# A third stack buffer, one merge transfer, a reordered sync queue, and rotary swaps issued by GpSimd

## What is computed

```python
x = x + tanh(g_xattn[0]) * xattn(layernorm(x), ctx_2048, ...)
x = x + tanh(g_ffn[0]) * ffn(layernorm(x), ...)

def xattn(x, c):                      # 16 batches of (128 channels, 512 positions)
    q, k, v = Wq @ x + bq, Wk @ c + bk, Wv @ c + bv      # 8 heads of 16 channels
    q, k = rope(q, 8), rope(k, 8)     # the first 8 channels of a head are rotated
    p = softmax(q.T @ k / sqrt(16))
    return Wo @ (p @ v) + bo

def ffn(x):                           # weights 4 bit, unpacked and scaled in the kernel
    gate, up = split(x @ w_gate_up.T)
    y = (silu(gate) * up) @ w_down.T
    return y / sqrt(mean(y * y) + 1e-6)
```

## Time and profile before

| | us |
|---|---|
| median of 3 runs | 921.22 |
| lowest and highest run | 918.21, 933.62 |
| the profiled execution | 918.37 |
| its span, first to last instruction | 916.6 |
| PE, DVE, ACT, POOL busy | 815.8, 522.1, 483.6, 178.5 |
| DMA engines' mean busy share | 33% |

### The profile page before, as it was taken

How to read it: one execution, slowest core, us unless ns; L and a number is a source line. 1 busy time by engine, 2 the same in 40 slices (tenths; PEclk the granted TensorE clock), 3 DMA queues, 4 the chain that set the end, 5 groups by cost and what they waited for, 6 DMA issues and landing times. The chain is left out here.

```text
span 916.6 us, 13653 instructions
## 1 busy us (share of the span) xinstructions
PE 815.8 (89%) x5110; PEld 421.6 (46%) x5142; DVE 522.1 (57%) x760; ACT 483.6 (53%) x895; POOL 178.5 (19%) x174
## 2 busy tenths in 40 slices
PE   3378999999998988999993599999999999999997
PEld 1123333333333333334332376666666666666664
DVE  4398977888987867888871961314131423141113
ACT  2227776887787766778792552325231623252223
POOL 1232333333333423331112820000000000000000
PEclk8559999999999988999996889999999999999999
DMA  5678555666665666465212010002000110000001
GB/s 167 171 198 218 155 142 153 189 200 194 170 165 152 175 175 189 119 167 153 69 33 79 8 46 1 1 1 67 25 1 1 47 45 0 0 27 21 0 1 46
DMA packets 55176, 86.44 MB, mean 94 GB/s; under 512 B 19274, under 2 KB 20938, under 8 KB 55114
## 3 DMA queue, kind: packets, MB, share of 16 engines
q1 hardware_dynamic: 55114, 85.62, 33.0%
HBM read 44.70 MB, written 34.34 MB: 86 GB/s over the span
## 5 line engine op out<-in xcount | busy, mean ns | idle before, releaser
L670 DVE TENSOR_REDUCE neg_max<-s_ps 128x2 f32<-128x1024 f32 x256 | 310.0, 1219 | 61.8 <-PE s_ps L420 60.8
L536 ACT ACTIVATE probs<-st_ps 128x512 f32<-128x512 f32 x512 | 277.9, 597 | 105.5 <-PE st_ps L432 101.2
L448 PE MATMUL pv_ps<-probs,v_ones 128*32 128x256 f32 x2048 | 166.1, 397 | 12.6 <-ACT pv_sb L542 12.6
L1098 PE MATMUL gu_ps<-x_head,gu_head 128*128 128x512 f32 x352 | 155.9, 443 | 0.0
L965 DVE TENSOR_TENSOR hidden<-gu_ps,silu 128x512 f32<-128x512 f32 x44 | 30.4, 691 | 202.6 <-ACT silu L1040 202.6
L420 PE MATMUL s_ps<-k_stack,q_stack 48*128 48x512 f32 x512 | 135.4, 526 | 10.5 <-DVE neg_max L670 8.4
L1099 PE MATMUL gu_ps<-x_rest,gu_head 128*128 128x512 f32 x352 | 139.0, 395 | 0.0
L1040 ACT ACTIVATE silu<-gu_ps 128x512 f32<-128x512 f32 x44 | 26.3, 597 | 204.8 <-PE gu_ps L1101 204.8
L432 PE MATMUL st_ps<-q_stack,k_stack 50*128 50x512 f32 x512 | 110.6, 421 | 12.9 <-DMA q_stack<-max_scratch 12.7
L420 PEld LDWEIGHTS s_ps<-k_stack,q_stack 48*128 48x128 f32 x512 | 50.4, 193 | 121.1 <-issue 81.1
L1115 PE MATMUL y_ps<-dn_head,h_head 128*128 128x512 f32 x176 | 101.5, 577 | 1.1 <-DVE h_rest L967 1.0
(11 more groups left out here) (114 smaller groups left out, 807.1 us busy)
## 6 DMA issues: line engine op xcount, KB each, us to landing
q_stack<-image SPq DMA_DIRECT2D x64, 192.0 KB, 3.9
k_stack<-image SPq DMA_DIRECT2D x64, 192.0 KB, 4.5
image<-split_head SPq DMA_DIRECT2D x32, 256.0 KB
image<-split_head SPq DMA_DIRECT2D x64, 128.0 KB
image<-split_rest SPq DMA_DIRECT2D x32, 256.0 KB
ct<-ctx_dram SPq DMA_DIRECT2D x16, 256.0 KB, 5.5
swap<-proj SPq DMA_DIRECT2D x64, 64.0 KB, 2.0
scale_of<-inverse_scratch SPq DMA_DIRECT2D x16, 256.0 KB
```

Of the source, the lines that this page charges most:

```text
L448: last = nc.tensor.matmul(pv_ps[2 * KC * j:2 * KC * (j + 1), cols], v_ones[b % 2][:, kt, j, quad, :], probs[at % PROBS][:, j, cols], start ...
L536: nc.scalar.activation(probs[at % PROBS][:, tile % 4, :], st_ps[item % ST_BANKS][:], ACT.Exp).then_inc(st_read, 1)
L670: nc.vector.tensor_reduce(neg_max[j // 2][:, :, j % 2, qt], s_ps[item % S_BANKS][:], AXIS_X, ALU.max, negate=True).then_inc(s_read, 1)
L1098: nc.tensor.matmul(gu_ps[t % 2][:, half], head, x_head[:, k], start=(k == 0), stop=False)
```

## The change

- `q_stack` and `k_stack` get three buffers (`STACKS`) instead of two. `load_stacks` reads a whole batch at once in four transfers of 384 KB, where `load_half` read 4 x 192 KB twice. It waits for all eight stores of its batch, and stands first in `sync_step` for batch b+2. It waits for the last `weigh` of batch b-1.
- The stores are `store_heads` (six transfers) and `store_rests` (two), both halves together. They stand at the end of `sync_step`, with `gather_sums(b, 0)` between them.
- On VectorE one cast of 128x1024 (`split_heads`, after slot 11) takes the place of `head_pass` (slot 7) and `head_rot` (slot 11); on GpSimd one subtract (`split_rests`) takes the place of two. `rotate` now leaves its result in `proj`, so `bias_rot` of the next batch waits for `rests`.
- The four swap transfers are issued by GpSimd in `pool_step`, after `residual` and before `rotate`.
- The rows of the two halves of the heads are interleaved, so `merge_quads` is one transfer over every second row instead of four, `store_inverse` one instead of two, and `load_inverse` two (one per half of the heads) instead of one.
- At the start, ScalarE does the scales, the gates and their table loads ahead of `bias_rot(2)`; GpSimd issues the first swaps once all constants are in, where SP issued them after the gates' transfers.

The core of the diff; `take_v`, `values`, `weigh`, `score` and the host's weight order only follow the new layout and buffer count.

```diff
-X_TILES, C_TILES, PROBS = 8, 4, 3
-MIX_AT, ROT_AT, PASS_AT, V_AT = 1, 2, 5, 8
+X_TILES, C_TILES, PROBS, STACKS = 8, 4, 3, 3
+MIX_AT, ROT_AT, PASS_AT, V_AT, HEADS_AT = 1, 2, 5, 8, 11
...
-            def swap_partners(sp, n):
-                sp.wait_ge(st_read, ST_NO["rot", n] + 1)
+            def swap_partners(pool, n):
+                pool.wait_ge(st_read, ST_NO["rot", n] + 1)
                 if n:
-                    sp.wait_ge(rot_rest, n)
+                    pool.wait_ge(rests, n)
                 for at in range(0, P, 64):
                     for to, source in ((at, at + 32), (at + 32, at)):
-                        sp.dma_start(swap[to:to + 32, :], proj[source:source + 32, 0, :]).then_inc(swapped, 16)
-
-            def store_head(sp, n, w):
-                sp.wait_ge((rot_head, pass_head)[w], n + 1)
-                rows = lambda first, count: image[n, first:first + STEP_ROWS * count:STEP_ROWS].rearrange("r h t -> r (h t)")
-                tile = split_head[:, w, :].bitcast(F32)
-                sp.dma_start(rows(3 * w + 1, 16), tile).then_inc(stored[w], 16)
-                sp.dma_start(rows(3 * w, 8), tile[halves[0]]).then_inc(stored[w], 16)
-                sp.dma_start(rows(K_ROW0 + 3 * w + 2, 8), tile[halves[1]]).then_inc(stored[w], 16)
-
-            def store_rest(sp, n, w):
-                sp.wait_ge((rot_rest, pass_rest)[w], n + 1)
-                rows = image[n, 3 * w + 2:3 * w + 2 + STEP_ROWS * 16:STEP_ROWS].rearrange("r h t -> r (h t)")
-                sp.dma_start(rows, split_rest[:, w, :].bitcast(F32)).then_inc(stored[w], 16)
-
-            def load_half(sp, n, h):
-                p = n % 2
+                        pool.dma_start(swap[to:to + 32, :], proj[source:source + 32, 0, :]).then_inc(swapped, 16)
+
+            def store_heads(sp, n):
+                sp.wait_ge(heads, n + 1)
+                tile = split_head[:].bitcast(F32)
                 for w in two:
-                    sp.wait_ge(stored[w], PARTS * (n + 1))
-                if n >= 2:
-                    sp.wait_ge(st_full, last_weight(n - 2, h))
+                    sp.dma_start(image_rows(n, 3 * w + 1, 16), tile[:, w, :]).then_inc(stored, 16)
+                    sp.dma_start(image_rows(n, 3 * w, 8), tile[halves[0], w, :]).then_inc(stored, 16)
+                    sp.dma_start(image_rows(n, K_ROW0 + 3 * w + 2, 8), tile[halves[1], w, :]).then_inc(stored, 16)
+
+            def store_rests(sp, n):
+                sp.wait_ge(rests, n + 1)
+                for w in two:
+                    sp.dma_start(image_rows(n, 3 * w + 2, 16), split_rest[:, w, :].bitcast(F32)).then_inc(stored, 16)
+
+            def load_stacks(sp, n):
+                sp.wait_ge(stored, PARTS * (n + 1))
+                if n >= STACKS:
+                    sp.wait_ge(st_full, last_weight(n - STACKS, 1))
                 for stack, row0 in ((q_stack, 0), (k_stack, K_ROW0)):
                     for odd in two:
-                        rows = stack[p][STACK * odd:STACK * odd + DATA_ROWS, columns(h), :].bitcast(F32)
-                        heads = slice(odd * PAIRS + 2 * h, odd * PAIRS + 2 * h + 2)
-                        sp.dma_start(rows, image[n, row0:row0 + DATA_ROWS, heads, :]).then_inc(half_in[p][h], 16)
+                        rows = stack[n % STACKS][STACK * odd:STACK * odd + DATA_ROWS, :, :].bitcast(F32)
+                        sp.dma_start(rows, image[n, row0:row0 + DATA_ROWS, odd * PAIRS:(odd + 1) * PAIRS, :]).then_inc(
+                            stack_in[n % STACKS], 16)
...
             def merge_quads(sp, b):
                 sp.wait_ge(sums_in[0], 16 * (b + 1))
-                for j in range(QUAD):
-                    rows = slice(2 * KC * j + KC, 2 * KC * (j + 1))
-                    sp.dma_start(pv_sb[0][b % 2][rows, :], pv_sb[1][b % 2][rows, :]).then_inc(merged[b % 2], 16)
+                sp.dma_start(pv_sb[0][b % 2][1:P:2, :], pv_sb[1][b % 2][1:P:2, :]).then_inc(merged[b % 2], 16)
 
             def store_inverse(sp, b):
                 sp.wait_ge(inverses, b + 1)
-                for h in two:
-                    sp.dma_start(inv_dram[b, :, h, :], sums[64 * h:64 * h + 64, :]).then_inc(inverse_out, 16)
+                sp.dma_start(inv_dram[b].rearrange("h j (x e) -> (h j x) e", e=32), sums[:]).then_inc(inverse_out, 16)
 
             def load_inverse(sp, b):
-                sp.wait_ge(inverse_out, 16 * QUADS * (b + 1))
+                sp.wait_ge(inverse_out, 16 * (b + 1))
                 if b:
                     sp.wait_ge(heads_ok, b)
-                sp.dma_start(scale_of[:], inv_dram[b].rearrange("j h t -> (j h) t").unsqueeze(1).to_broadcast(
-                    [HEADS, KC, T])).then_inc(inverse_in, 16)
+                for h in two:
+                    sp.dma_start(scale_of[h:P:2, :], inv_dram[b, h].unsqueeze(1).to_broadcast([QUAD, KC, T])).then_inc(inverse_in, 16)
...
             def sync_step(sp, b):
                 nxt, proj_n = b + 1 < B, b + AHEAD_PROJ
-                if nxt:
-                    load_half(sp, b + 1, 1)
+                if b + 2 < B:
+                    load_stacks(sp, b + 2)
                 store_max(sp, b, 1)
-                if proj_n < B:
-                    swap_partners(sp, proj_n)
                 if b:
                     gather_sums(sp, b - 1, 1)
+                load_max(sp, b, 1)
+                if b:
                     merge_quads(sp, b - 1)
-                load_max(sp, b, 1)
                 if b >= 2:
                     store_x(sp, b - 2)
                 if b:
                     store_inverse(sp, b - 1)
-                if proj_n < B:
-                    store_head(sp, proj_n, 1)
-                if b + 2 < B:
-                    load_half(sp, b + 2, 0)
                 if nxt:
                     store_max(sp, b + 1, 0)
+                if b + 5 < B:
+                    load_inputs(sp, b + 5)
                 if b:
                     load_inverse(sp, b - 1)
-                if proj_n < B:
-                    store_rest(sp, proj_n, 1)
-                if b + 5 < B:
-                    load_inputs(sp, b + 5)
                 if nxt:
                     load_max(sp, b + 1, 0)
+                if proj_n < B:
+                    store_heads(sp, proj_n)
                 gather_sums(sp, b, 0)
                 if proj_n < B:
-                    store_head(sp, proj_n, 0)
-                    store_rest(sp, proj_n, 0)
+                    store_rests(sp, proj_n)
...
-                swap_partners(sp, 0)
                 sp.dma_start(gu_sc16[:], d["gate_up_scales"].rearrange("g (t o) -> (g t) o", o=P)).then_inc(scales_in, 16)
                 sp.dma_start(dn_sc16[:], d["down_scales"].rearrange("g (t o) -> (g t) o", o=P)).then_inc(scales_in, 16)
-                store_head(sp, 0, 1)
-                store_rest(sp, 0, 1)
-                store_head(sp, 0, 0)
-                store_rest(sp, 0, 0)
-                sp.wait_ge(ones_set, 2)
-                for h in two:
-                    load_half(sp, 0, h)
-                swap_partners(sp, 1)
+                store_heads(sp, 0)
+                store_rests(sp, 0)
+                sp.wait_ge(ones_set, STACKS)
+                load_stacks(sp, 0)
                 load_inputs(sp, 3)
-                for w in (1, 0):
-                    store_head(sp, 1, w)
-                    store_rest(sp, 1, w)
-                load_half(sp, 1, 0)
+                store_heads(sp, 1)
+                store_rests(sp, 1)
+                load_stacks(sp, 1)
                 store_max(sp, 0, 0)
-                swap_partners(sp, 2)
                 load_max(sp, 0, 0)
                 load_inputs(sp, 4)
-                for w in (1, 0):
-                    store_head(sp, 2, w)
-                    store_rest(sp, 2, w)
+                store_heads(sp, 2)
+                store_rests(sp, 2)
...
-                engine.wait_ge(rot_head, n + 1)
+                ops.tensor_tensor(proj[:, 0], swap[:], turned[:], ALU.add).then_inc(rotated, 1)
+
+            def split_rests(engine, ops, n):
+                engine.wait_ge(heads, n + 1)
                 if n:
-                    engine.wait_ge(stored[0], PARTS * n)
-                ops.tensor_tensor(split_rest[:, 0], swap[:], split_head[:, 0].bitcast(F32), ALU.subtract).then_inc(rot_rest, 1)
-
-            def rest_pass(engine, ops, n):
-                engine.wait_ge(pass_head, n + 1)
-                if n:
-                    engine.wait_ge(stored[1], PARTS * n)
-                ops.tensor_tensor(split_rest[:, 1], proj[:, 1], split_head[:, 1].bitcast(F32), ALU.subtract).then_inc(pass_rest, 1)
+                    engine.wait_ge(stored, PARTS * n)
+                ops.tensor_tensor(split_rest[:], proj[:], split_head[:].bitcast(F32), ALU.subtract).then_inc(rests, 1)
...
+            def split_heads(dve, n):
+                dve.wait_ge(st_read, ST_NO["pass", n] + 1)
                 dve.wait_ge(rotated, n + 1)
                 if n:
-                    dve.wait_ge(stored[0], PARTS * n)
```

(24 more changed lines are left out.)

93 lines of the change are left out of this document (42 added, 51 removed).

## The result

The changed kernel takes 1013.5 us (median of 4 runs, 1005.4 to 1015.9) where the kernel before takes 919.7 beside it. The ratio is 1.101, with a 95% interval of 1.093 to 1.109: 94 us slower. The forecast was 938 us, in a range of 904 to 958.

The account below looks back on a forecast made before the run. It took TensorE's waits at S for the maxima (16 us) and the slow clock behind them (9 us) as the prize; -25 + 19.5 + 11 + 13.5 + 1 = +20 us on 918.4 gave 938, range 904 to 958.

Parts of the forecast that it names:

- The wait at S goes: At S, where TensorE starts `weigh` slot 0, its wait for `load_max(b+1, 0)` goes: -25 us, clock included.
- The price of the load: `load_stacks`: a full 1.5 MB stack takes 9.1 us, as read from the start of the program.
- Rival B: `load_stacks` in `sync_step` takes 7.6 us, lands in time and no step waits: 905 us; chance 0.26.
- When the load starts: Head of a step: the eight stores end, and the stack load starts, 3.8 us into the next step.
- The wait at slot 6: VectorE's `invert_sums` waits for `gather_sums` behind the load: 1.5 us in each of steps 1 to 13, 19.5 us.
- The clock: Behind thirteen waits near 1.5 us, five drops to the lower clock at the mean 2.2 us: 11 us.
- The start: Start through `weigh` slot 8 of step 0: 11.5 us later, 2 more for the clock: +13.5 us.
- GpSimd's swaps hidden: GpSimd issues four swaps at 0.62 us each; the rotation ends by S + 13.0, ahead of the merged cast.
- Tail: End of the kernel: the last scale tile's transfer is partly bandwidth; bounds 0 and +1.7, taken as +1 us.
- The third buffer cannot help: In the start, what is late is not a free buffer but the 1.5 MB ahead of a 16 KB row.
- Rival C: GpSimd's swap issue takes 3.2 us each, delaying the start and the merged cast: 973 us; chance 0.07.
- rival D: `load_max(b+1, 0)` lands after S + 26.8, so the 25 us do not come back: 955 to 965; chance 0.10.

Follow-up runs that it names:

- e16: e11 with the second half of stack b+2 loaded behind load_inverse(b-1), not right behind the first half; 892.2 us, ratio 0.965.
- e11: Kernel before with GpSimd-issued swaps, three stack buffers, both halves of stack b+2 loaded behind load_max(b, 1), load_max(b+1, 0) ahead of load_inverse; 907.4 us.
- e1: Kernel after with the stack load cut by columns into 8 transfers with rows of 4 KB, in the same place; 1008.8 us, ratio 1.087.
- e3: Kernel after with the stack load behind load_max(b, 1) and cut into rows of 4 KB; 914.5 us, ratio 0.989.
- e13: e3 with five extra VectorE products of 0.7 us at slot 0 of steps 1 to 13; 938.8 us.
- e7: e3 with two extra VectorE products of 0.7 us at slot 6 of steps 1 to 13; 990.7 us.
- e5: Kernel before with the swaps issued by GpSimd ahead of its rotation, in the start ahead of its wait for constants; 917.6 us, ratio 0.995.
- e4: Kernel after with the swaps issued by SP again, behind store_max(b, 1) and, in the start, in their old places; 1014.2 us, ratio 1.094.
- e2: Kernel after with load_stacks(b+2) issued behind load_max(b, 1), not at the head of the step; 930.9 us, ratio 1.003.
- e15: e11 with the output projection of stage b-2 behind slot 4 instead of slot 1; 917.0 us, ratio 0.995.
- e14: e3 with five extra VectorE products of 0.7 us at slot 12 of steps 1 to 13; 1018.5 us.
- e6: Kernel after with gather_sums(b-1, 1) issued by GpSimd behind the swaps, not by SP behind the stack load; 1020.9 us.

## Why the prediction was wrong, point by point

- **The wait at S goes, -25 us**. Right: from step 1 to step 13 no wait of TensorE for `max_scratch` is left. e16 shows that a step without waits is 25.3 us.
- **The price of the load, 9.1 us.** Wrong: 11.8. I took it from the one full stack of the start and from another form of the load. The place alone does not explain it, since the first load of the kernel after, in the start, takes 11.6 already. e11 has the form of before for a whole stack: 9.1 us for the first, in the start, and 10.1 in the median from step 0 on. So of the 2.7 us some 1.0 is the loop and some 1.7 the new form; of that the longer rows are 0.5 (e1, e3), and the rest, the order of the transfers or what runs beside them, is open. The half stacks in the loop of the kernel before take 6.5 us in the median; less the 2.0 of a small transfer that makes 2.0 + 2 x 4.5 = 11.0. Those transfers stood in the same trace, and I did not use them. Rival B bet on the other sign (8 KB rows quicker) at 0.26; e1 and e3 show them slower.
- **When the load starts, S + 3.8.** About right: S + 3.1 in step 7. Over steps 1 to 13 it was S - 0.1 to S + 6.0, and where it was at S (steps 1 and 8) `invert_sums` did not wait.
- **The wait at slot 6, 1.5 us in steps 1 to 13.** Right in place and in the instruction. It came in eleven of the thirteen steps, and the size was 3.25 us in step 7 and 4.0 in the mean (54.8 less the 10.6 and a 0.3 at the stage's end). TensorE's waits at the v projection make 47.6 us where the sum had 19.5.
- **The clock, five drops at 2.2 us = 11 us. This is the step that failed.** By the estimate above the lower clock cost 53 us. Three faults in it. The price came from pauses at S, and was used for waits at slot 6, behind which TensorE pauses at slot 8. Before, the lower clock was over by S + 7 each time; after, ten of the eleven pauses at slot 8 of steps 2 to 13 brought 7 to 27 us of it. The share, four of seven, came from the same place; at slot 8 it was nearly every one. And four of seven, for thirteen waits, are seven drops and 16 us; the five of the sum had no reason. e13 against e7 shows that the place makes a difference. With 53 us there instead of 11, and 45 of waiting at mid-step instead of 19.5, the sum for the steps would have been -25 + 45 + 53 = +73, where 69.0 were measured.
- **The start, +13.5 us.** Measured +25.8. The first score came at 45.1, not 41.0, and slot 8 of step 0 at 96.7, not 89.2. The three loads ahead took 11.6, 11.8 and 12.2 us (6.0 more than the 9.1, 9.1 and 11.4 of the sum), stores and casts the rest of the 7.5. From there to S of step 1 another 6.9 us were lost, TensorE being at half clock all the while, where I had 2. So the price of the load and that of the clock make up most of it. In e5 GpSimd issues the first swaps ahead of its wait for the constants, and the first weigh comes 6 us earlier than before, not later.
- **GpSimd's swaps hidden.** Right as to time (e4, e5). Their landing took 7.5 us and not 2.0, beside the load (2.3 in e2, where the load stands elsewhere); in step 7 the rotation ended at S + 19.0, not 13.0, and its cast came at S + 27 with the slower step.
- **Tail, +1.** Nothing in the whole: 477.6 us behind S of step 14 in both. The last scale tile took 5.1 us from its issue to the product (584.51 to 589.63) against 3.7, +1.5, which something ahead of it gave back; that it was the single transfers for the sums and the merge is not shown. The Trainium skill ("DMA: Bandwidth & Descriptors", Rules for kernel authors) says that an outermost dimension under 16 keeps a transfer on at most so many engines, by which I had estimated +1.7; the +1.5 is near it, and no run here tests the number of engines by itself.
- **The third buffer cannot help.** True of the order that the change has, too narrow as a statement. It frees the load from its place: e2, e3, e11 and e16 load a stack a whole step ahead, which two buffers do not allow.
- **Rival C** (GpSimd's issue dear) and **rival D** (the wait at S stays) did not occur. The forecast named two durations as its weak point. One of them was; the clock, which I had given 11 us and no bound of its own, was the larger.

What stays open: why a pause at slot 3 leaves the clock up and one at slot 8 mostly does not, and why the price of one at slot 8 varies from nothing to 27 us. The rows show only what TensorE does around them. The output and input projections run in slots 1 to 5, and stretches at half clock that began in one step and reached into the next ended there at S + 1.5 to S + 7.2; in e15, with the output projection at slot 4, at S + 7.9 to S + 9.1. But nine of the kernel after's ended in the middle of a step, at S + 23.9 to S + 33.5, where no such projection runs, so this cannot be the whole. In e13 the one pause that did bring half clock, 6.8 us of it, was that of step 13, the first without an input projection; it was also the longest:

```profile
434.36 0.79 PE L404 MATMUL s_ps<-k_stack,q_stack 48*128 48x512 f32 x2 [3.08 <-DVE neg_max L641]
```

None of this was tested.

## What to carry to other kernels

Price a wait by where TensorE would pause: take the lower clock behind it from rows of a pause at the same place in the loop, and if there is none, give it a wide bound: here the same pause cost nothing at one slot and up to 27 us at half clock at another. Nothing small that is wanted soon should be issued behind a large load, on any queue; a further buffer is worth what the queue's order makes of it. Take the duration of a transfer from the loop and from one of the same form; here each of the two was worth 1 us or more.

## What the runs showed of the hardware

- The clock's price depended on place: no half clock behind twelve pauses of 1.7 to 2.1 us at slot 3 (e13), 10.2 us with each of thirteen of 2.7 to 5.0 us at slot 15 (e14), 3.4 to 27.3 us behind twelve of thirteen pauses of 1.5 to 3.3 us at slot 8 (e7's profile). In ten of e7's twelve stretches TensorE was busy without a break.
- An 8 KB transfer that GpSimd issued beside a 1.5 MB load from SP took 8.6 us (one step of e6), and the 64 KB swaps 7.5 us in the median (kernel after), against 2.3 where the load stood elsewhere (e2).
- The same 1.5 MB took 11.8 us as four transfers with rows of 8 KB (kernel after), 11.0 to 11.4 as eight with rows of 4 KB (e3, e1), and 10.1 as eight in the order of the kernel before, first halves first (e11, where other transfers run beside it).
